# A fused transformer layer on eight cores: the residual and layernorm between attention and FFN moved from the attention loop into a stage of its own, and the FFN's weight buffers and matmul order changed

## The reference, cut to what matters

```python
def attn(x, W_spin, b_spin, W_global, W_J, beta):
    s = jnp.einsum('bni,oi->bno', x, W_spin) + b_spin
    mean_field = jnp.mean(s, axis=1, keepdims=True)
    global_influence = jnp.einsum('bmd,od->bmo', mean_field, W_global)
    energy_fields = jnp.einsum('bnd,od->bno', s, W_J)
    scores = jnp.einsum('bnd,bmd->bnm', energy_fields, s) / sqrt(1024)
    local_field = jnp.einsum('bnm,bmd->bnd', softmax(scores), s)
    return jnp.tanh(beta * (s + global_influence + local_field))

def ffn(x, w_gate, w_up, w_down):      # int32 weights, scaled by 1/127
    h = jax.nn.silu(x @ wg.T) * (x @ wu.T)
    return h @ wd.T

x = x + layernorm(attn(layernorm(x)))   # x: (4, 4096, 1024), float32
x = x + layernorm(ffn(layernorm(x)))    # hidden width 3072
```

## Time and profile before

| | |
|---|---|
| timed runs of the kernel before | 1410.18 and 1581.2 us (median 1495.69 us) |
| profiled execution, its own time | 1411.23 us |
| its span on the slowest core (core 3) | 1409.7 us; all cores 1390.3 to 1409.7 us |
| PE busy in the span | 1183.2 us (84%) |
| DVE, ACT, POOL busy | 374.6 (27%), 246.3 (17%), 73.1 us (5%) |
| mean granted TensorE clock, by core | 0.940 to 0.944 |

### The profile page before, as it was taken

How to read it: one execution, slowest core, us unless ns; L and a number is a source line. 1 busy time by engine, 2 the same in 40 slices (tenths; PEclk the granted TensorE clock), 3 DMA queues, 4 the chain that set the end, 5 groups by cost and what they waited for, 6 DMA issues and landing times.

```text
span 1409.7 us, 14562 instructions; the slowest of 8 cores (1390.3 to 1409.7 us)
## 1 busy us (share of the span) xinstructions
PE 1183.2 (84%) x5274; PEld 512.9 (36%) x5274; DVE 374.6 (27%) x620; ACT 246.3 (17%) x371; POOL 73.1 (5%) x92
## 2 busy tenths in 40 slices
PE   0787887879999999999999011399999999999997
PEld 0232332223444444444444000144444444444443
DVE  2243433301133223222322311121112111134343
ACT  0111111211132324223332100011111111100000
POOL 0011110000000000000000100011111110000000
PEclk9998998999999999999999555599999999999999
DMA  9746655772134432432342655573737454023332
GB/s 191 155 110 135 142 131 138 152 142 50 38 67 101 97 72 67 113 90 68 85 101 62 105 119 118 109 86 31 90 32 89 39 64 47 1 90 92 117 90 89
DMA packets 228341, 131.01 MB, mean 93 GB/s; under 512 B 204720, under 2 KB 204720, under 8 KB 228272
## 3 DMA queue, kind: packets, MB, share of 16 engines
q1 hardware_dynamic: 102944, 83.94, 23.7%
q0 software_dynamic: 57744, 29.37, 16.0%
q10 hardware_dynamic: 67584, 16.79, 6.7%
HBM read 96.51 MB, written 20.97 MB: 83 GB/s over the span
## 4 chain that ended last, share of the span: by engine, by line
PE 75%; DMA 14%; DVE 4%; issue 2%; SPq 2%; ACT 1%; ACTq 1%; DVEq 0%
PE ps_pv L732 15%; PE ps_q L624 14%; PE ps_d L1099 12%; PE ps_g L956 12%; PE ps_u L968 11%; PE ps_s L258 6%; DMA xnT_sb<-xn_bf 6%; DMA x1r<-x_sc 5%; PE ps_e L307 3%; SPq L894 1%; PE ps_s L254 1%; DMA PT_sb<-P_sb 1%; PE ps_pv L435 1%; DVE xn_bf L880 1%; DMA s_FM<-s_tok 1%
## 5 line engine op out<-in xcount | busy, mean ns | idle before, releaser
L956 PE MATMUL ps_g<-xn2T,wg_sb 128*128 128x512 bf16 x768 | 188.1, 389 | 118.1 <-DMA xn2T<-xn_bf 118.1
L624 PE MATMUL ps_q<-s_FM,ebuf 128*128 128x512 bf16 x1024 | 225.6, 381 | 8.6 <-DMA ebuf<-e_sc 8.6
L732 PE MATMUL ps_pv<-s_tok,PT_sb 128*128 128x512 bf16 x1024 | 227.8, 383 | 3.9 <-DMA PT_sb<-P_sb 3.0
L968 PE MATMUL ps_u<-xn2T,wu_sb 128*128 128x512 bf16 x768 | 182.5, 381 | 0.0
L1099 PE MATMUL ps_d<-wdT_sb,h_act 128*128 128x512 bf16 x768 | 165.9, 379 | 1.0 <-DVE h_act L991 1.0
L956 PEld LDWEIGHTS ps_g<-xn2T,wg_sb 128*128 128x128 bf16 x768 | 76.2, 100 | 213.4 <-issue 126.6
L624 PEld LDWEIGHTS ps_q<-s_FM,ebuf 128*128 128x128 bf16 x1024 | 100.2, 98 | 131.3 <-issue 12.3
L732 PEld LDWEIGHTS ps_pv<-s_tok,PT_sb 128*128 128x128 bf16 x1024 | 100.5, 99 | 128.5 <-issue 11.9
L258 PE MATMUL ps_s<-wspT_sb,xnT_sb 128*128 128x512 bf16 x512 | 135.7, 412 | 0.0
L991 DVE SCALAR_TENSOR_TENSOR h_act<-silu_b,ps_u 128x512 bf16<-128x512 f32 x96 | 65.8, 687 | 261.5 <-PE ps_u L968 261.5
L981 ACT ACTIVATE silu_b<-ps_g 128x512 f32<-128x512 f32 x96 | 57.3, 597 | 341.6 <-PE ps_g L956 341.5
(11 more groups left out here) (67 smaller groups left out, 462.8 us busy)
## 6 DMA issues: line engine op xcount, KB each, us to landing
xs<-x SPq DMA_DIRECT2D x16, 1024.0 KB, 6.4
xs2c<-x SPq DMA_DIRECT2D x16, 512.0 KB, 5.2
x_sc<-x1c SPq DMA_DIRECT2D x16, 512.0 KB, 3.2
x1r<-x_sc SPq DMA_DIRECT2D x16, 512.0 KB, 4.1
xs<-x_sc SPq DMA_DIRECT2D x16, 512.0 KB, 4.5
out<-out_b SPq DMA_DIRECT2D x16, 512.0 KB, 5.3
wg_sb<-wgT POOLq DMA_DIRECT2D x24, 256.0 KB, 5.0
wu_sb<-wuT POOLq DMA_DIRECT2D x24, 256.0 KB, 5.8
```

What stands on the lines that cost most here:

```text
L624: i = t.matmul(ps_q[:, slot, half * 512:(half + 1) * 512], ebuf[:, qt % 2, j, :], s_FM[:, j, qi * 1024 + half * 512: qi * 1024 + (half + 1 ...
L732: i = t.matmul(ps_pv2[:, nb * 512:(nb + 1) * 512], PT_sb[:, par, cb * P:(cb + 1) * P], s_tok[:, cb, nb * 512:(nb + 1) * 512], start=(cb == ...
L956: i = t.matmul(ps_g[:, slot, :], wg_sb[:, par, j, :], xn2T[:, j, tb * 512:(tb + 1) * 512], start=(j == 0), stop=(j == KC - 1))
L968: i = t.matmul(ps_u[:, slot, :], wu_sb[:, par, j, :], xn2T[:, j, tb * 512:(tb + 1) * 512], start=(j == 0), stop=(j == KC - 1))
```

## The change

Seven things change together.

- `emit_xld` and `emit_l2c` are gone from the attention loop. ACT instead writes the tanh result attn_wb to DRAM (`fdma`, attn_sc).
- The bridge does the whole of it: SP loads chunks of two tiles, attn_sc and x (`l2_chunk`, two chunks in buffers). DVE normalizes, adds, takes statistics (`l2_grpA`), and ACT writes x1 to x_sc and takes the square root. Then DVE takes the reciprocal and applies the second layernorm (`l2_grpB`), and SP transposes. `l2_grpB` of a tile stands behind `l2_grpA` of the next one.
- The 16 square roots of the first of these layernorms are one ACT instruction ahead of the bridge (`l2_s0`).
- P_sb holds four quarters: the exp of a quarter waits for the transpose of the same quarter of the tile before.
- The FFN makes all four gate groups of a hidden block and then all four up groups.
- The FFN's weights have two slots instead of four and are loaded two blocks ahead, each behind the last up matmul of the block that used the slot. silu_b has two slots.
- tmp2 takes the second DVE sum in stage C, where tmp1 was overwritten, and wglT_sb and P_sb move to the other side of SBUF.

```diff
-        P_sb = eC(nc.sbuf_tensor("P_sb", [P, 2, 1024], BF16, side="right"))
+        P_sb = eC(nc.sbuf_tensor("P_sb", [P, N], BF16))
+        tmp2 = eC(nc.sbuf_tensor("tmp2", [P, D], F32))
-        def emit_xld(t, wv_war):
...
             def fexp(s, qt=qt, qi=qi, slot=slot, cp=cp,
                      wt=rec[("scq", qt, qi)],
-                     wtr=(rec.get(("ptr", qt, qi - 2), 0) if qi >= 2
-                          else rec.get(("ptr", qt - 1, qi + 2), 0)),
+                     wtr=rec.get(("ptr", qt - 1, qi), 0),
                      wrs=rec.get(("rsfix", qt - 1), 0)):
                 s.wait_ge(st.h, wt)
-                s.activation(out=P_sb[:, qi % 2, :],
+                s.activation(out=P_sb[:, qi * 1024:(qi + 1) * 1024],
                              in_=ps_q[:, slot, :], func=AF.Exp,
...
-                i = v.tensor_tensor(out=tmp1[:], in0=tmp1[:],
+                i = v.tensor_tensor(out=tmp2[:], in0=tmp1[:],
                                     in1=s_tok[:, qt, :], op=ALU.add)
...
-                    wd=rec.get(("l2app", qt - 2), 0)):
+                    wd=rec.get(("attn_dma", qt - 2), 0)):
-                    s.wait_ge(sv.h, wd)
-                s.activation(out=attn_wb[:, par, :], in_=tmp1[:],
+                    s.wait_ge(wd[0].h, wd[1])
+                s.activation(out=attn_wb[:, par, :], in_=tmp2[:],
                              func=AF.Tanh, scale=beta_col[:]
                              ).then_inc(ss.h, 1)
...
-            if qt >= 1:
-                emit_l2c(qt - 1)
-            if qt == NT_OWN - 1:
-                emit_l2c(qt)
+
+            def fdma(s, qt=qt, par=par, wss=rec[("tanh", qt)]):
+                s.wait_ge(ss.h, wss)
+                s.dma_start(out=attn_d.rearrange("(q p) d -> q p d", p=P)[qt],
+                            in_=attn_wb[:, par, :]).then_inc(dsm[qt % 2].h, 16)
+            s_add(fdma)
+            dsm[qt % 2].n += 16
+            rec[("attn_dma", qt)] = (dsm[qt % 2], dsm[qt % 2].n)
...
-            nc.sbuf_tensor("wg_sb", [P, 4, KC, P], BF16, side="right"))
+            nc.sbuf_tensor("wg_sb", [P, 2, KC, P], BF16, side="right"))
-            nc.sbuf_tensor("wu_sb", [P, 4, KC, P], BF16, side="right"))
+            nc.sbuf_tensor("wu_sb", [P, 2, KC, P], BF16, side="right"))
-            nc.sbuf_tensor("silu_b", [P, 4, 512], F32, side="right"))
+            nc.sbuf_tensor("silu_b", [P, 2, 512], F32, side="right"))
...
-        x1r = e2(nc.sbuf_tensor("x1r", [P, 2, D], F32))
+        xs2 = e2(nc.sbuf_tensor("xs2", [P, 2, 2, D], F32))
+        ab_buf = e2(nc.sbuf_tensor("ab_buf", [P, 2, 2, D], BF16))
+        ln_tmp = e2(nc.sbuf_tensor("ln_tmp", [P, 2, D], F32))
+        x1_buf = e2(nc.sbuf_tensor("x1_buf", [P, 2, D], F32))
...
+        def l2_s0(s):
             s.wait_ge(sv.h, pc_done["sv"])
-            i = s.activation(out=sqv3[:], in_=mvb3_all[:, :, 1], func=AF.Sqrt,
-                             scale=c_sc127[:], bias=c_b127[:])
+            i = s.activation(out=sq2_all[:], in_=mv2_all[:, :, 1], func=AF.Sqrt,
+                             bias=eps_col[:])
             vinc(ss, i)
...
+        def l2_chunk(c):
+            sem = da[c % 2]
+            w0 = rec[("attn_dma", 2 * c)]
+            w1 = rec[("attn_dma", 2 * c + 1)]
+            w2 = rec.get(("l2_lastread", c - 2), 0)
+            first = (c <= 1)
...
+                if w2:
+                    sync.wait_ge(sv.h, w2)
+                sync.dma_start(out=ab_buf[:, c % 2], in_=attn_r[c]
+                               ).then_inc(sem.h, 16)
+                sync.dma_start(out=xs2[:, c % 2], in_=x_own_r[c]
+                               ).then_inc(sem.h, 16)
+            block.sync(f)
+            sem.n += 32
+            rec[("l2chunk", c)] = (sem, sem.n)
+        l2_chunk(0)
+        l2_chunk(1)
...
+        def l2_grpA(t_i):
+            c, par = t_i // 2, t_i % 2
+            w_sq = rec.get(("sq3", t_i - 2), 0)
...
+            def fv1(v, t_i=t_i, c=c, par=par, w_sq=w_sq):
+                w = rec[("l2chunk", c)]
+                v.wait_ge(w[0].h, w[1])
+                v.wait_ge(sv.h, sv_l2s)
+                if w_sq:
+                    v.wait_ge(ss.h, w_sq)
+                i = v.tensor_scalar(out=ln_tmp[:, par, :],
+                                    in0=ab_buf[:, c % 2, t_i % 2, :],
+                                    scalar1=mv2_all[:, t_i, 0:1],
+                                    scalar2=rs2_all[:, t_i:t_i + 1],
+                                    op0=ALU.subtract, op1=ALU.mult)
+                vinc(sv, i)
+                v.wait_ge(sv.h, sv.n)
+                if t_i >= 2:
+                    w = rec[("x1_dma", t_i - 2)]
+                    v.wait_ge(w[0].h, w[1])
+                i = v.tensor_tensor(out=x1_buf[:, par, :], in0=ln_tmp[:, par, :],
+                                    in1=xs2[:, c % 2, t_i % 2, :], op=ALU.add)
...
+            rec[("x1", t_i)] = sv.n
+
+            def fdma2(s, t_i=t_i, par=par, wv=sv.n):
+                s.wait_ge(sv.h, wv)
+                s.dma_start(out=x1_d.rearrange("(q p) d -> q p d", p=P)[t_i],
+                            in_=x1_buf[:, par, :]).then_inc(dtm[t_i % 2].h, 16)
+            s_add(fdma2)
+            dtm[t_i % 2].n += 16
+            rec[("x1_dma", t_i)] = (dtm[t_i % 2], dtm[t_i % 2].n)
+            def fs2b(s, t_i=t_i, par=par, wv=sv.n):
+                s.wait_ge(sv.h, wv)
+                s.activation(out=sqv2[:, par, :], in_=mvb2[:, par, 1:2],
+                             func=AF.Sqrt, scale=c_sc127[:], bias=c_b127[:]
+                             ).then_inc(ss.h, 1)
+            s_add(fs2b)
+            ss.n += 1
+            rec[("sq3", t_i)] = ss.n
+            if t_i % 2 == 1:
+                rec[("l2_lastread", c)] = rec[("x1", t_i)]
+                if c + 2 < NT_OWN // 2:
+                    l2_chunk(c + 2)
...
+        def l2_grpB(t_i):
...
+            def fv2b(v, t_i=t_i, par=par):
+                v.wait_ge(ss.h, rec[("sq3", t_i)])
+                i = v.reciprocal(out=rsig2[:, par, :], in_=sqv2[:, par, :])
+                vinc(sv, i)
+                v.wait_ge(sv.h, sv.n)
...
-                i = v.tensor_scalar(out=xn2_bf[:, par, :], in0=x1r[:, par, :],
-                                    scalar1=mvb3_all[:, t_i, 0:1],
...
+                i = v.tensor_scalar(out=xn2_bf[:, par, :], in0=x1_buf[:, par, :],
+                                    scalar1=mvb2[:, par, 0:1],
+                                    scalar2=rsig2[:, par, :],
                                     op0=ALU.subtract, op1=ALU.mult)
                 vinc(sv, i)
...
+        for t_i in range(NT_OWN + 1):
+            if t_i < NT_OWN:
+                l2_grpA(t_i)
+            if t_i >= 1:
+                l2_grpB(t_i - 1)
+        s_flush()
...
+        def ffn_wload(hb):
+            sem = dwP[hb % 2]
+            par = hb % 2
+            w_war = rec.get(("up_mm", hb - 2, 3), 0)
+            first = (hb <= 1)
...
-        def ffn_group(k, hb, tb, slot, sbs, w4=None):
...
-        ffn_wload(2)
         for hb in range(HC):
+            par = hb % 2
             for tb in range(4):
-                ffn_group(hb, hb, tb, tb, tb,
-                          w4=(rec[("xtr4", tb)] if hb == 0 else None))
-            if hb + 3 < HC:
-                ffn_wload(hb + 3)
+                def ftg(t, hb=hb, par=par, tb=tb, w4=rec[("xtr4", tb)]):
+                    if tb == 0:
+                        w = rec[("wload", hb)]
+                        t.wait_ge(w[0].h, w[1])
...
+                    if hb >= 1:
+                        t.wait_ge(ss.h, rec[("silu", hb - 1, tb)])
+                    for j in range(KC):
+                        i = t.matmul(ps_g[:, tb, :], wg_sb[:, par, j, :],
+                                     xn2T[:, j, tb * 512:(tb + 1) * 512],
+                                     start=(j == 0), stop=(j == KC - 1))
...
+            for tb in range(4):
+                def ftu(t, hb=hb, par=par, tb=tb):
+                    if hb >= 1:
+                        t.wait_ge(sv.h, rec[("hmul", hb - 1, tb)])
...
+            for tb in range(4):
+                prev_h = (rec.get(("hmul", hb, tb - 2), 0) if tb >= 2
+                          else rec.get(("hmul", hb - 1, tb + 2), 0))
+
+                def fsl(s, hb=hb, tb=tb, wt=rec[("g_mm", hb, tb)], prev=prev_h):
+                    s.wait_ge(st.h, wt)
+                    if prev:
+                        s.wait_ge(sv.h, prev)
+                    s.activation(out=silu_b[:, tb % 2, :], in_=ps_g[:, tb, :],
...
+            if hb + 2 < HC:
+                ffn_wload(hb + 2)
```

More of the change, by code:

```diff
@@ new lines, in build_program, with l2_v0, f @@
+        block.scalar(l2_s0)
+        ss_sq2 = ss.n
+        def l2_v0(v):
+            v.wait_ge(ss.h, ss_sq2)
+            i = v.reciprocal(out=rs2_all[:], in_=sq2_all[:])
+            vinc(sv, i)
+        block.vector(l2_v0)
+        sv_l2s = sv.n
+        attn_r = attn_d.rearrange("(c t p) d -> c p t d", t=2, p=P)
```

(45 more changed lines are left out.)

248 lines of the change are left out of this document (45 added, 203 removed).

## The result

The changed kernel takes 1385.43 us (median of 10 runs) against 1408.21 us before (8 runs). The ratio is 0.983, interval 0.981 to 0.985: about 24 us less, where the forecast was 12 less; the time itself lies inside the stated range. Runs in which one die ran at a lower clock are left out of every ratio here; the medians of times contain them. The profiled execution took 1387.33 us, its slowest core is core 7 with a span of 1385.8.

A forecast was written before the change was run, and what follows sets the result against it. The prediction saw PE bounding stages C and D and a latency chain bounding the old bridge, with DMA limiting the new one. 1411.2 - 4.6 (stage C) - 12.6 (bridge) + 5.2 (FFN) = 1399.2 us; range 1376 to 1426.

The forecast's parts named there:

- Stage C: End of the attention loop: the last tile's 64 PV matmuls no longer wait for late transposes, -4.6 us.
- the two reasons I named: Last tile of stage C: nothing ahead of the transposes in SP's queue, and a P_sb slot per quarter; together 4.6 us.
- FFN: First hidden block: three additional up groups remain after the last transposed tiles arrive, 3 x 1.73, +5.2 us.
- the rival of late weights: FFN: weights queued behind four large down-weight loads come about 7 us late each time, 28 us, total 1427 us; chance 0.06.
- Bridge: Last tile's statistics in stage C to the last waiting gate group: 128.9 becomes 116.3 us, -12.6, with DMA as the limit.
- start: Bridge: the first chunk's load beside the weights, 1.57 MB at 180 GB/s plus latency and sharing, 13 us; ends 8 and 20.
- pace x 16: Bridge: 16 tiles limited by DMA at 6.25 us each, the middle of 5.35 and 7.15, 100 us.
- the lower end: Bridge DMA rate: 220 GB/s with transposes in between, at a share of 1.10, giving 7.15 us a tile.
- The upper end: Bridge DMA rate: stage D's 106 GB/s at share 0.36 scaled to 294 when full, giving 5.35 us a tile.
- the first rival: Bridge: DVE is the limit at 4.96 us a tile, total 1378.6 us, 2.3% faster; chance 0.17.
- DVE-bound: Bridge: DVE instructions follow one another without waits, 4.96 us a tile, total 1378.6 us; chance 0.17.
- Blocked queue: Bridge: loads and transposes block each other in SP's queue, stopping DVE and emptying DMA; 8.74 us a tile, 1439 us; chance 0.19.

The follow-up runs named there:

- SP's order alone: Kernel before with only stage C's x1 store and x load moved behind the next tile's transposes in SP's queue: ratio 0.996, stage C 467.0 against 473.1 us.
- the alternating order: Changed kernel with the FFN's matmuls again in the order gate, up, gate, up: ratio 0.983, measured again 0.981 beside the changed kernel's 0.986.
- the square of runs: Changed kernel, and it without the second BN_STATS (0.983), without x loads of chunks 2 to 7 (0.977), and without both (0.974).
- the run with late weights: Changed kernel with the first two pairs of FFN weight loads held until DVE finished the first half of bridge tile 9: ratio 0.985.

## Why the prediction was half the gain

**Stage C: right.** -4.6 was forecast, -5.9 (change) and -6.1 (SP's order alone) measured. The last 64 matmuls took 13.98 us for the 13.8 worked out, 4.4 less than the 18.4 before; the other 1.5 us of the median no run explains. Of the two reasons I named, the queue's order does it; the slots of P_sb could have been left out.

**FFN: right.** From the last waiting gate group to the next block's first on core 7 it is 891.77 - 881.42 = 10.35 us, where it was 5.2: +5.15 for a forecast of 5.2.

```profile
881.42 3.57 PE L976 MATMUL ps_g<-xn2T,wg_sb 128*128 128x512 bf16 x8 [10.79 <-DMA xn2T<-xn_bf]
...
884.79 7.14 PE L987 MATMUL ps_u<-xn2T,wu_sb 128*128 128x512 bf16 x32
...
891.77 0.59 PE L976 MATMUL ps_g<-xn2T,wg_sb 128*128 128x512 bf16 x2
```

Two weight slots cost nothing, as said (324.4 us in the alternating order with two, 324.3 before with four), and the rival of late weights never came up.

**Bridge: the DMA side as the limit right, two terms mis-sized.** By the same marks as the forecast, on core 7:

| term | forecast | measured |
|---|---|---|
| start | 13 | 786.34 - 777.23 = 9.1 |
| pace x 16 | 6.25 x 16 = 100 | 877.74 - 786.34 = 91.4, 5.71 a tile |
| end | 3.3 | 881.42 - 877.74 = 3.7 |
| sum | 116.3 | 104.2 |

The step that failed is the choice of the rate: "Both are above DVE's 4.96, so I take the DMA as the limit and the middle of the two, 6.25 us". That is 1.57 MB at about 252 GB/s for every one of the 16 tiles. The runs show 5.71 us instead, at a mean of 271 GB/s, and not as an even rate: DVE does most tiles in 4.86 us and stands still for 14.1 us in sum, 10.2 of them for transposes. That the DMA side makes these waits is shown by the square of runs. That 271 GB/s is a ceiling is not shown: single slices of 5 us reach 385 and 395. What misled me is the lower end: the 220 GB/s of the earlier trace rows was taken as a full engine with transposes, since its share was 1.10. The changed bridge has the same share of 1.10 at 271, and the old bridge with four slots of x1r 1.18 at 238. A share says that packets are open, not how fast they pass, so it can't turn a rate into a ceiling. The upper end (294 at share 1) was the nearer one, but it came from the same scaling, so that was luck. The start failed in the same way: the chunk was priced at 180 GB/s, the rate of one row with the weights open, and from 778 to 802, with them open again, the engines moved 245 GB/s. "Some delay from sharing" was not the error: it was priced at about 1.5 us, and the run with late weights took 1.2 off the start. -3.9 for the start, -8.6 for the pace and +0.4 for the end make the 12.1 us between forecast and result in the bridge. In the whole time the forecast was 13.8 us too high; 3.0 of them are its base, a profiled execution of 1411.2 where the median before is 1408.2.

The Trainium skill, page "DMA: Bandwidth & Descriptors", section "Bandwidth", gives a core about 358 GB/s with its neighbour streaming too. The trace does not reach it as a sustained rate, 271 over 80 us, though single slices of 5 us pass it (395). Had I taken it, DVE would have been the bound, and the result near the first rival's.

**The rivals.** DVE-bound (1378.6 us): as a time it was nearer than the forecast, 6.8 us under the result where the forecast was 13.8 above, but it is not what happened: less DVE work brought 0.4 us. It applies once the bridge is 9 us shorter. Blocked queue (1439): as a time it is refuted. Its first half is seen in small: late transposes stop DVE for 10.2 us in two times, and after the second stop the share falls to 0.68 for one slice. But the place in SP's queue is not the reason, since taking the chunks out of it made these waits 22.8. The Trainium skill, same page, section "Queues, rings and completion order", has a DMA engine going round-robin between queues, in order within one. By that rule transposes in a queue of their own would no longer stand behind a chunk's descriptors and should have come earlier; in this case they came no earlier (7.7 us against 6.0), though the chunks now shared a queue with ACT's stores as well.

**Too narrow a look at the alternatives.** The prediction called the old bridge a chain of latencies and then priced only the change's way out of it, which doubles the bytes per tile. The other way, more loads under way with half the bytes, has a bridge 28 to 30 us shorter.

## What to carry to other kernels

When a stretch has no full engine, find its chain and deepen it first; moving work into it traded a latency for bytes here, and the work that was hidden under a PE-bound stage had better been left there. Take a DMA rate as a ceiling only from a stretch in which something waits for the DMA all the time with several transfers queued: a low rate beside a high share did not mean full engines here, and by this test the 271 GB/s of the changed bridge is no ceiling either. For the last turn of a software pipeline look at what stands ahead in the in-order queues, since nothing covers it there.
